# Softmax attention: the first two score tiles move to the end of the sequence before, the projections one place back

## The reference, cut to what matters

```python
# L1 ("causal"): rotary queries and keys, causal mask
q = frac_rope(x @ wq) * D ** -0.5
k = frac_rope(x @ wk) * D ** -0.5
s = q @ k.T - NEG * (i < j)
out = softmax(s) @ (x @ wv) @ wo

# L3 ("relu"): projections with bias and relu, all 512 keys of a sequence
q, k, v = relu(x @ Wq + bq), relu(x @ Wk + bk), relu(x @ Wv + bv)
e = q @ k.T / sqrt(D) - 1e4 * causal
y = relu(softmax(e) @ v @ Wo + bo)
```

## Time and profile before

| | us |
|---|---|
| median of 3 executions | 4512.2 (4511.21 to 4512.94) |
| the profiled execution | 4524.18 |
| its span | 4522.3 |
| causal phase, first to last instruction | 3536.7 to 3676.9 |
| relu phase, first to last instruction | 4207.7 to 4350.4 |

### The profile page before, as it was taken

How to read it: one execution, slowest core, us unless ns; L and a number is a source line. 1 busy time by engine, 2 the same in 40 slices (tenths; PEclk the granted TensorE clock), 3 DMA queues, 4 the chain that set the end, 5 groups by cost and what they waited for, 6 DMA issues and landing times. The chain is left out here.

```text
span 4522.3 us, 165982 instructions
## 1 busy us (share of the span) xinstructions
PE 4022.2 (89%) x70454; PEld 3247.3 (72%) x70454; DVE 3109.3 (69%) x5297; ACT 2597.1 (57%) x4169; POOL 2416.1 (53%) x1973
## 2 busy tenths in 40 slices
PE   6896999999999999999999999999999767667666
PEld 5885777777777777777777777777777447557456
DVE  4556777877788777877778777777776463273452
ACT  3333666566665666666666666666665436555445
POOL 3335666656666566656665666656654117516126
PEclk9997999999999999999999999999999878868878
DMA  1003222232222222222222322222222021312122
GB/s 27 0 0 88 66 72 68 58 86 75 69 68 79 73 69 70 68 79 72 72 68 74 76 73 65 70 63 75 65 71 52 10 63 44 79 55 53 32 67 80
DMA packets 214404, 281.81 MB, mean 62 GB/s; under 512 B 58942, under 2 KB 103908, under 8 KB 212932
## 3 DMA queue, kind: packets, MB, share of 16 engines
q1 hardware_dynamic: 199940, 249.88, 20.9%
q0 software_dynamic: 9536, 19.55, 1.6%
q10 hardware_dynamic: 4224, 2.10, 0.2%
HBM read 55.01 MB, written 18.28 MB: 16 GB/s over the span
## 5 line engine op out<-in xcount | busy, mean ns | idle before, releaser
L1709 POOL TENSOR_TENSOR local_normed<-local_rot,local_sines 128x512 f32<-128x512 f32 x768 | 954.0, 1278 | 781.4 <-PE local_bank L1417 776.8
L1719 POOL TENSOR_TENSOR local_normed<-local_normed,local_inv_norm 128x1024 f32<-128x1024 f32 x384 | 733.9, 1933 | 260.1 <-ACT local_inv_norm L1609 260.1
L1786 DVE TENSOR_TENSOR local_rot<-local_bank,local_table 128x1024 f32<-128x1024 f32 x384 | 470.3, 1225 | 333.7 <-ACT local_squares L1590 327.0
L1334 PE MATMUL local_bank<-local_wqkv_hi,local_ys_hi 128*128 128x512 f32 x1152 | 501.1, 435 | 36.6 <-issue 24.8
L1786 DVE TENSOR_TENSOR local_sines<-local_bank,local_table 128x1024 f32<-128x1024 f32 x384 | 466.4, 1215 | 0.0
L1792 DVE TENSOR_REDUCE local_norm<-local_squares 128x16 f32<-128x1024 f32 x384 | 464.1, 1209 | 0.0
L1336 PE MATMUL local_bank<-local_wqkv_hi,local_ys_lo 128*128 128x512 f32 x1152 | 457.8, 397 | 0.0
L1335 PE MATMUL local_bank<-local_wqkv_lo,local_ys_hi 128*128 128x512 f32 x1152 | 455.9, 396 | 0.5 <-issue 0.5
L1590 ACT ACTIVATE local_squares<-local_bank 128x1024 f32<-128x1024 f32 x384 | 396.0, 1032 | 102.0 <-PE local_bank L1336 102.0
L1585 ACT COPY local_v_tile<-local_bank 128x1024 f32<-128x1024 f32 x192 | 194.8, 1014 | 395.2 <-PE local_bank L1336 395.1
L1773 DVE TENSOR_REDUCE local_top<-local_bank 128x16 f32<-128x1024 f32 x192 | 234.8, 1223 | 266.9 <-PE local_bank L1365 266.6
(11 more groups left out here) (400 smaller groups left out, 8076.3 us busy)
## 6 DMA issues: line engine op xcount, KB each, us to landing
local_vals<-local_v_tile SPq DMA_DIRECT2D x1152, 130.0 KB
local_vals<-local_v_tile SPq DMA_DIRECT2D x672, 65.0 KB
local_stage<-in_L_ffn_Wqkv SPq DMA_DIRECT2D x6, 1536.0 KB
moe_w<-in_L_ffn_W SPq DMA_DIRECT2D x3, 2048.0 KB, 10.0
x_rows<-moe_rows SPq DMA_DIRECT2D x24, 256.0 KB, 4.9
moe_w<-y_rows SPq DMA_DIRECT2D x24, 256.0 KB, 5.1
local_wo<-in_L_ffn_Wo SPq DMA_DIRECT2D x6, 512.0 KB, 8.2
moe_taken<-x_rows,moe_take POOLq DMA_INDIRECT x149, 2.6
```

What stands on the lines that cost most here:

```text
L1334: nc.tensor.matmul(out, hi, wqkv_hi[:, d0:d1], start=True, stop=False)
L1709: last = nc.gpsimd.tensor_tensor(of_heads(normed, a)[:, :, to], of_heads(rot, a)[:, :, to], of_heads(sines, a)[:, :, of], ALU.add)
L1719: nc.gpsimd.tensor_tensor(of_heads(normed, a), of_heads(normed, a), inv_norm[:, a * HEADS:(a + 1) * HEADS].unsqueeze(2).to_broadcast([P, H ...
L1786: last = nc.vector.tensor_tensor(of_heads(out, a), src, table[:, m % TILES, row, :].unsqueeze(1).to_broadcast([P, HEADS, HD]), ALU.mult)
```

## The change

The helpers stay as they are; the loops of three engines call them in another order. `scores(s + 1, 0)` and `scores(s + 1, 1)` with their `centre` and `exponentials` stand at the end of iteration `s`, not at the start of iteration `s + 1`: for the first sequence they stand in iteration -1. On TensorE each projection stands one place later: `project_q` behind `scores(s, 2)`, `project_k` behind `scores(s, 3)`, `project_v` behind `turn(s, 2)`, `project_values` behind `turn(s, 3)`. On ScalarE `copy_probs_t(s, 2)` stands before `value` and `normalise`, and `query` and `key` keep their place after a copy of probabilities. On VectorE `centre(s, 2)` stands before `row_stats(s + 2)`, and `centre(s, 3)` before `row_shift` and the products for k. No instruction is added or taken away.

```diff
--- before.py
+++ after.py
@@ -712,30 +712,30 @@
                     if s == -1:
                         act.wait_ge(q["loaded"], LOADS)
                     if is_seq(s):
-                        exponentials(s, 0)
-                        exponentials(s, 1)
+                        copy_probs_t(s, 0)
                     if is_seq(s + 1) and not rope:
                         query(s + 1)
                     if is_seq(s):
-                        copy_probs_t(s, 0)
                         exponentials(s, 2)
+                        copy_probs_t(s, 1)
                     if is_seq(s + 1) and not rope:
                         key(s + 1)
                     if is_seq(s):
-                        copy_probs_t(s, 1)
                         exponentials(s, 3)
+                        copy_probs_t(s, 2)
                     if is_seq(s + 1):
                         value(s + 1)
                     if is_seq(s + 2):
                         normalise(s + 2)
                     if is_seq(s):
-                        copy_probs_t(s, 2)
+                        copy_probs_t(s, 3)
                     if is_seq(s + 1):
                         value_out(s + 1)
-                    if is_seq(s):
-                        copy_probs_t(s, 3)
+                        exponentials(s + 1, 0)
                     if is_seq(s + 2):
                         copy_rows(s + 2)
+                    if is_seq(s + 1):
+                        exponentials(s + 1, 1)
 
             @block.tensor
             def _(pe):
@@ -809,35 +809,35 @@
                         if rope:
                             pe.wait_ge(q["rot_ready"], 1)
                     if is_seq(s):
-                        scores(s, 0)
-                        scores(s, 1)
-                    if is_seq(s + 1):
-                        project_q(s + 1)
-                    if is_seq(s):
                         turn(s, 0)
                         scores(s, 2)
                     if is_seq(s + 1):
-                        project_k(s + 1)
+                        project_q(s + 1)
                     if is_seq(s):
                         weigh(s, 0)
                         turn(s, 1)
                         scores(s, 3)
                     if is_seq(s + 1):
+                        project_k(s + 1)
+                    if is_seq(s):
+                        weigh(s, 1)
+                        turn(s, 2)
+                    if is_seq(s + 1):
                         if rope:
                             project_k_rot(s + 1)
                         project_v(s + 1)
                     if is_seq(s):
-                        weigh(s, 1)
-                        turn(s, 2)
+                        weigh(s, 2)
+                        turn(s, 3)
                     if is_seq(s + 1):
                         project_values(s + 1)
+                        scores(s + 1, 0)
                     if is_seq(s):
-                        weigh(s, 2)
-                        turn(s, 3)
+                        weigh(s, 3)
                     if is_seq(s + 2):
                         turn_rows(s + 2)
-                    if is_seq(s):
-                        weigh(s, 3)
+                    if is_seq(s + 1):
+                        scores(s + 1, 1)
 
             @block.gpsimd
             def _(pool):
@@ -922,24 +922,27 @@
                         if rope:
                             turn_weights()
                     if is_seq(s):
-                        centre(s, 0)
-                        centre(s, 1)
+                        centre(s, 2)
                     if is_seq(s + 2):
                         row_stats(s + 2)
                     if is_seq(s + 1) and rope:
                         rope_products(s + 1, "q", q_t, 0)
                     if is_seq(s):
-                        centre(s, 2)
                         add_output(s, 0)
+                        centre(s, 3)
                     if is_seq(s + 2):
                         row_shift(s + 2)
                     if is_seq(s + 1) and rope:
                         rope_products(s + 1, "k", k_t, 1)
                     if is_seq(s):
-                        centre(s, 3)
                         add_output(s, 1)
                         add_output(s, 2)
+                    if is_seq(s + 1):
+                        centre(s + 1, 0)
+                    if is_seq(s):
                         add_output(s, 3)
+                    if is_seq(s + 1):
+                        centre(s + 1, 1)
 
     run_phase(nc, name, body)
```

## The result

The changed kernel takes 4471.5 us (median of 4 runs, 4464.52 to 4480.57) beside 4512.1 for the kernel before on the same chip: a ratio of 0.9907 with the interval [0.9894, 0.9920]. Two later comparisons gave 0.9899 [0.9882, 0.9915] and 0.9908 [0.9891, 0.9924]. It is 40.6 us faster by the medians, where 42.4 were forecast; in the two later comparisons the medians differ by 45.8 and 43.0.

What follows compares the result with a forecast made beforehand. TensorE, nearest to full but waiting on chains through VectorE and ScalarE, was taken as the bound. Gains of 17.7 (relu), 23.6 (causal) and 1.1 (start and end), 42.4 us, take 4512.2 to 4469.8; forecast 4470, range 4460 to 4490.

Steps and rivals of the forecast that it cites:

- Relu's interval, 13.7: Relu time per sequence falls from 16.39 to 13.7 us: work 12.66, waits 0.83, 0.1 for waiting loads, joints.
- the work of 12.66: TensorE's own work in one relu sequence, summed from distances between instruction starts: 12.66 us.
- the 0.83 us of waits: Relu, TensorE before `turn` and `weigh` of tile 0: chain of 3.85 us less 3.02 of work beside it.
- for joints that I can't see: Allowance in relu's interval for unseen gaps: 13.6 us was taken as 13.7.
- Covers: Relu: TensorE work hides the chains to `weigh` of tile 2 (3.91 over 3.85) and tile 3 (3.93 over 3.80).
- the late queue: Rival: `row_stats` on VectorE delays chains to `weigh` of tile 2; 14 intervals lose 1.4 us each, 4489 us; chance 0.12.
- Causal's interval, 12.3: Causal time per sequence becomes 11.9 to 12.4 us, taken as 12.3; chain to `weigh` of tile 2 even at 8.4.
- The clock, 4.9 us: Causal: four of seven intervals lose about 1.2 us each to the lower clock; none expected afterwards, 4.9 us in all.
- the forecast's own sign of being wrong: Granted clock below 0.95 in either phase behind the first sequence; also a wait over 0.5 us before another `weigh`.
- Start and end: First `turn` earlier by 2.4 us causal, 0.4 relu; last sequence loses 0.83 per phase; together +1.1 us won.
- Sum: Gain over both phases: relu 17.7, causal 23.6, start and end 1.1, together 42.4 us.
- The rival with a time of 4423: TensorE isn't the floor, VectorE is: 9.94 us in relu, 9.25 in causal; 89 us won; chance 0.03.

Runs made afterwards that it cites:

- e7: Changed kernel, relu only: both next-sequence score tiles earlier on TensorE, `centre` of tile 1 before `add_output` on VectorE; 4477.0 us (1 run), relu interval 13.15.
- e4: Changed kernel with the four row-statistics instructions done twice, the first into an unused tile; 4471.4 us (1 run), intervals 12.93 causal, 14.31 relu.
- e5: Kernel before with the causal transposes of tile 2 issued five times instead of once; 4508.2 us (1 run).
- e11: Kernel before with only the score tiles moved, plus the causal transposes of tile 2 issued five times; 4503.4 us (1 run).
- e2: Kernel before with only the later projections, earlier copy of tile 2's probabilities and earlier `centre` of tiles 2 and 3; 4485.5 us, ratio 0.9948.
- e12: Kernel before, unchanged, profiled a second time; 4511.7 us (1 run).
- e10: Changed kernel itself, timed and profiled again without edits; 4475.0 us, ratio 0.9908 to the kernel before.
- e8: Changed kernel, causal only: `row_shift` behind the q products, `normalise` and `copy_probs_t(s, 2)` ahead of `exponentials(s, 3)`; 4468.4 us (1 run), causal interval 11.79.
- e9: Changed kernel with the edits of e7 and e8 together; 4460.9 us, ratio 0.9878 to the kernel before.

## Why the prediction was right

- *Relu's interval, 13.7.* Measured 13.68: the work of 12.66 held (e7), the 0.83 us of waits is 0.77 and the longer passes behind them 0.16 (0.1 forecast), and 0.09 is the `weigh` of tile 2, 0.98 for 0.89. The 0.1 "for joints that I can't see" came to the same, by luck.
- *Covers.* Before the value product and the `weigh` of tile 3 nothing shows in relu, as forecast, and at tile 2 only the 0.09. The cover there was given as 0.06 and is 0.15 by e4, so the late queue was a near rival, not a remote one: 0.8 us more in VectorE's queue cost 0.6 per interval in relu and 0.4 in causal.
- *Causal's interval, 12.3.* Measured 12.52, and the last 11.42 (11.5). The step that was off is the chain. The one to the `weigh` of tile 2 was worked out as even, 8.4 us beside 8.4, and e4 bears it out. The one to tile 3 decides, by a wait of 0.54 us; it was worked out for relu and not for causal. The working gave 11.9 as the lower bound, and the 12.3 taken above it came from no row: that it lies within 0.22 of the measured interval is luck. Over seven intervals that is 86.6 - 85.3 = 1.3 us less won.
- *The clock, 4.9 us.* Shown by e5 (4.75 won against the first profile of before, 3.5 against the second) and e11. Between the first and the last first turn it doesn't fall in any profile of the change. Behind the last one it does: the forecast's own sign of being wrong, a granted clock below 0.95 behind the first sequence, was met there, and so was another one, a wait of over 0.5 us before another `weigh`: 1.90 us at tile 2. It fell there before as well, so the difference of the two kernels hardly shows it. The Trainium skill, page "TensorE: Matmul & The Clock Gate", section "A second HAM failure mode: psum-queue depth-cycling", lets short idle times swing the clock. The loops with waits of 1.58 and 0.75 us and of 0.74 and 0.85 us agree, though only in some intervals; e2 with its 1.5 us doesn't show it, nor do the waits left in the changed loops, 0.54 us or less. The forecast's argument that relu holds 1.00 with waits up to 0.8 us was wrong: relu before falls in e12 and e5.
- *Start and end.* Start -2.03 and -1.27 (forecast -2.4 and -0.4), where profiles of one code differ by up to 0.9. End +0.68 and +0.79 (+0.83 each); in causal +0.83 where both are at full clock (e12, e10).
- *Sum.* 42.2 in the two phases beside 42.4. That this is within 0.2 is partly luck: causal's seven intervals gave 1.3 less than forecast, relu's gave 18.06 for 17.7, and starts and ends gave 1.8 for 1.1. Not seen: relu before sometimes has falls as well, three in e12, 3.7 us, which the change then wins too; that pair of profiles gives 45.0.
- *TensorE as the floor.* The rival with a time of 4423 fell: in e8 and e9 TensorE is busy for the whole causal interval, 11.79, and VectorE for 9.40 of it. The Trainium skill, page "Perfetto Trace Analysis", section "Identifying the Most-Contended Engine", wants the share of the peak FLOP rate and the weight loads in place of matmul busy time. They are 7.44 of those 11.79 us, and the interval went no lower.

## What to carry to other kernels

In a loop over several engines, add for every waiting instruction its chain and TensorE's work beside it, in each variant of the loop, and don't stop at the first chain that comes out even. A delay at one wait is partly taken off the next (e4). Two reorderings that each close one of two chains won more together than apart here, and one alone won nothing. If waits of TensorE precede a lower clock, a test with repeated, unneeded work in their place prices the clock by itself. Look at the last turn of the loop too: there the work that covers the waits is missing.

## What was not expected of the hardware

- More work made a phase faster: 12 extra transposes per sequence took 3.5 to 4.75 us (e5) and 5.76 us (e11) off the causal phase.
- The same relu code took 16.39 or 17.64 us a sequence, alternating (e12), with the granted clock at 1.00 or 0.90, while the loop whose longest wait was 1.5 us, once per sequence (e2), held 1.00 throughout.
- The causal phase, behind the same instructions, began between 3516.7 and 3536.8 us in the fourteen profiles, so the total of a single run can't judge an edit of a few us. The interval can: the causal one of the changed kernel was 12.52 in each of four profiles.
